# Table rows read two at a time and elsewhere, a fixed buffer for a chunk's first unit, and one instruction for two one-hots, in a two-layer graph network kernel

## The reference

```python
def _sage_conv(x, src, dst, W_l, b_l, W_r):
    msgs = x[src]
    agg = jax.ops.segment_sum(msgs, dst, num_segments=N_NODES)   # 12500 nodes
    deg = jax.ops.segment_sum(jnp.ones((src.shape[0],), x.dtype), dst, num_segments=N_NODES)
    mean = agg / jnp.maximum(deg, 1.0)[:, None]
    return mean @ W_l + b_l + x @ W_r
h = relu(_sage_conv(x, src, dst, W1_l, b1, W1_r))
h = relu(_sage_conv(h, src, dst, W2_l, b2, W2_r))
out = layernorm(x + h @ W3 + b3)
```

## Time and profile before

| | |
|---|---|
| Runs | 3, 3705.2 to 3718.2 us, median 3707.2 |
| The profiled execution | 3708.1 us; its span, first to last instruction, 3706.3 |
| TensorE | matmuls 2906.8 us (78%), weight loads 2393.2 (65%) |
| VectorE | 1475.7 us (40%), 3568 instructions |
| GpSimd | 2397.0 us (65%), 2448 of them gathers |
| ScalarE | 483.7 us (13%) |
| DMA | 653 MB, mean 176 GB/s |
| Granted TensorE clock | 0.897 of full speed over the span |

### The profile page before, as it was taken

How to read it: one execution, slowest core, us unless ns; L and a number is a source line. 1 busy time by engine, 2 the same in 40 slices (tenths; PEclk the granted TensorE clock), 3 DMA queues, 4 the chain that set the end, 5 groups by cost and what they waited for, 6 DMA issues and landing times.

```text
span 3706.3 us, 65299 instructions
## 1 busy us (share of the span) xinstructions
PE 2906.8 (78%) x13209; PEld 2393.2 (65%) x13210; DVE 1475.7 (40%) x3568; ACT 483.7 (13%) x1411; POOL 2397.0 (65%) x2455
## 2 busy tenths in 40 slices
PE   4777778788877878879865676888887888888866
PEld 2455667566656656768754565777776777777755
DVE  6555455445544444443222222333333333333332
ACT  2000000000000000010100111111112121121112
POOL 2556566556655666567655577777777777777765
PEclk7788899889989999989987888999999999999988
DMA  3234565557456556657655444776775766767665
GB/s 84 87 109 132 172 209 175 169 165 225 131 178 187 173 176 208 192 171 217 203 170 157 124 121 127 208 216 180 208 225 171 213 201 195 222 180 217 201 186 159
DMA packets 496459, 653.03 MB, mean 176 GB/s; under 512 B 184190, under 2 KB 414580, under 8 KB 493142
## 3 DMA queue, kind: packets, MB, share of 16 engines
q0 software_dynamic: 117504, 321.02, 29.4%
q1 hardware_dynamic: 298038, 254.08, 22.4%
q10 hardware_dynamic: 80800, 76.82, 6.8%
HBM read 581.29 MB, written 70.40 MB: 176 GB/s over the span
## 4 chain that ended last, share of the span: by engine, by line
PE 30%; POOL 21%; issue 16%; DVEq 12%; DMA 10%; DVE 6%; ACT 2%; PEld 1%; SPq 1%; PEldq 1%; ACTq 0%; POOLq 0%
POOL ring L406 21%; PE ps L486 15%; PE ps L545 7%; PE psY L588 3%; DMA counts<-scratch 3%; DMA ring<-z_rows,scol 3%; DVEq L886 2%; PE psY L577 2%; DVE oh L905 2%; DVEq L917 1%; DVE oh L907 1%; DMA scratch<-in_x 1%; DVE oh L874 1%; DMA work<-in_x 1%; DMA scratch<-z_rows 1%
## 5 line engine op out<-in xcount | busy, mean ns | idle before, releaser
L486 PE MATMUL ps<-ring,oh 128*125 128x257 f32 (+1 forms) x6416 | 1677.6, 417 | 501.0 <-DMA ring<-z_rows,scol 170.0
L486 PEld LDWEIGHTS ps<-ring,oh 128*125 128x125 f32 x6416 | 1291.0, 206 | 810.3 <-issue 597.8
L406 POOL DMA_INDIRECT ring<-in_x,scol x1224 | 1194.3, 976 | 850.9 <-PE ps L486 510.7
L406 POOL DMA_INDIRECT ring<-z_rows,scol x1224 | 1202.0, 982 | 435.3 <-issue 358.8
L874 DVE SCALAR_TENSOR_TENSOR oh<-dcol,cf,iota 128x500 f32<-128x500 int16 x802 | 594.1, 741 | 1319.3 <-PE ps L486 893.8
L545 PE MATMUL ps<-scratch 128*125 128x257 f32 (+1 forms) x2000 | 485.4, 391 | 14.0 <-DMA scratch<-in_x 14.0
L545 PEld LDWEIGHTS ps<-scratch 128*125 128x125 f32 x2000 | 460.4, 295 | 32.8 <-DMA scratch<-in_x 17.3
L861 DVE TENSOR_TENSOR acc<-ps,acc x806 | 337.3, 418 | 19.3 <-issue 15.3
L516 PE MATMUL psB<-oh 128*128 x540 | 180.2, 429 | 176.7 <-DVE oh L907 173.1
L1152 ACT COPY work<-psY 125x256 f32<-125x256 f32 x100 | 37.2, 372 | 1570.3 <-PE psY L577 1570.3
L516 PEld LDWEIGHTS psB<-oh 128*128 x540 | 53.7, 99 | 291.1 <-issue 267.2
(11 more groups left out here) (118 smaller groups left out, 1178.2 us busy)
## 6 DMA issues: line engine op xcount, KB each, us to landing
scratch<-counts SPq DMA_DIRECT2D x200, 312.5 KB
scratch<-in_x SPq DMA_DIRECT2D x114, 512.0 KB, 4.1
scratch<-z_rows SPq DMA_DIRECT2D x114, 512.0 KB, 4.3
counts<-scratch SPq DMA_DIRECT2D x25, 1250.0 KB
work<-in_x ACTq DMA_DIRECT2D x200, 125.0 KB
ring<-in_x,scol POOLq DMA_INDIRECT x1224
ring<-z_rows,scol POOLq DMA_INDIRECT x1224
scratch<-in_x SPq DMA_DIRECT2D x114, 128.0 KB, 6.4
```

Source lines behind the costliest of these rows:

```text
L406: pool.indirect_dma_start(ring[:, slot, b, 0:D], None, rows_dram, bass.IndirectOffsetOnAxis(scol[:, n - C0:n - C0 + 1], 0)).then_inc(rows[ ...
L486: mm = pe.matmul(psA[0:WN, bass.ds(bank, W)], oh[:, 2 * (slot % 2) + later, b, :], ring[:, slot, b, 0:W], start=(b == 0), stop=(b == nb - 1))
```

## The change

- `tab` has the words (first, lo = first + 1, end, until). The constant `blk` and its DMA are gone: the column is worked out from `ga` or `gb`. VectorE's setup has one more instruction of 306 words.
- A load brings eight words, the rows of two groups next to each other. `front` (groups i = 0 and 2) is loaded for the next four in group i = 3, `back` (i = 3 and 1) in group i = 0. The loads stand between the one-hot and the add on VectorE, and behind a group's first four products on TensorE. The `reg_add` to `lo` is gone.
- A chunk's row of `tabh` is loaded (`chunk_row`) in the group ahead of it, at the same place, instead of in `chunk`. The first chunks of a window have theirs ahead of `chunk` as before.
- SLOTS is 3. A chunk's first unit always uses place 0, without a wait. Later units use places 2 and 1 in turn (the counter is the loop's), and wait until all but the last unit have been multiplied (`s_cnt` starts at 2 and not at 4).
- One `tensor_tensor` over 2 x 128 columns makes both one-hots of 128, instead of two `tensor_scalar`. The two of 500 stay.
- The word of `win` for the next window is loaded at the end of `dense1`, and in `dense2` behind line 1022, instead of at their heads.

The diff, cut to its core (TensorE's `four_rows`, `row_of` and `chunk_row` are as VectorE's):

```diff
-SLOTS = 4
+SLOTS = 3
-            sp.dma_start(tab, c_tab).then_inc(s_w, 16)
...
+            def group(l, i, nb, builds=False):        # TensorE
+                lo, hi = row_of(i)[1:3]
+                pe.wait_ge(rows[l][i], pe.snap(turn, min_val=16, max_val=16 * GB * NGG))
+                pair(l, i, nb, 0)
+                if i == 0:
+                    four_rows(back, gb)
+                    pe.reg_add(gb, gb, -8)
+                if i == 3:
+                    pe.reg_add(ga, ga, 8)
+                    four_rows(front, ga)
+                if builds:
+                    chunk_row()
                 with pe.If(pe.snap(lo) < pe.snap(hi)):
                     with pe.Fori(pe.snap(lo, min_val=1, max_val=NW), pe.snap(hi, min_val=1, max_val=NW)):
-                        pair(l, slot, nb, 1)
-                pe.reg_add(gi, gi, -4 if i % 2 else 4)
+                        pair(l, i, nb, 1)
...
             def chunk(n):
-                pe.load([more], tabh[0:1, bass.ds(pe.snap(at_row, min_val=1, max_val=2 * (NH + NW) - 1), 1)])
-                pe.reg_add(at_row, at_row, 2)
-                count_blocks(n, True)
+                count_blocks(n, True, 0)
                 with pe.If(1 < pe.snap(more)):
-                    with pe.Fori(1, pe.snap(more, min_val=1, max_val=HB)):
-                        count_blocks(n, False)
+                    with pe.Fori(1, pe.snap(more, min_val=1, max_val=HB)) as j:
+                        pe.reg_alu(slot_at, j, 1, ALU.bitwise_and)
+                        pe.reg_alu(slot_at, slot_at, SW, ALU.mult)
+                        count_blocks(n, False, pe.snap(slot_at, min_val=0, max_val=SW) + SW)
...
+            def four_rows(row, at):                   # VectorE
+                v.load(row, tab[0:1, bass.ds(v.snap(at, min_val=0, max_val=(NGG - 2) * 4), 8)])
+            def row_of(i):
+                return (front[0:4], back[4:8], front[4:8], back[0:4])[i]
+            def mark_groups(l, i, nb, w, later, free):
                 at = (2 * (i % 2) + later) * OH
-                v.wait_ge(s_mm[l], v.snap(free, min_val=1, max_val=NG * NW + 2))
+                g = (ga, gb)[i % 2]
+                blk = v.snap(g, min_val=0, max_val=(NGG - 2) * 4) + (G0 * GB - C0 + (4 if i in (1, 2) else 0))
+                v.wait_ge(s_mm[l], free)
                 v.scalar_tensor_tensor(
...
-                add_product(l)
-                step(w)
-            def group(l, i, nb):
-                gi = (ga, gb)[i % 2]
-                v.load([first, hi, until, blk], tab[0:1, bass.ds(v.snap(gi, min_val=0, max_val=(NGG - 1) * 4), 4)])
-                v.reg_add(lo, first, 1)
-                pair(l, i, nb, v.snap(first, min_val=0, max_val=NW - 1), 0, c)
+            def group(l, i, nb, builds=False):
+                first, lo, hi, _ = row_of(i)
+                cv = v.snap(c, min_val=1, max_val=NG * NW + 1)
+                mark_groups(l, i, nb, v.snap(first, min_val=0, max_val=NW - 1), 0, cv)
+                if i == 0:
+                    four_rows(back, gb)
+                if i == 3:
+                    v.reg_add(ga, ga, 8)
+                    four_rows(front, ga)
+                if builds:
+                    chunk_row()
+                add_product(l, cv)
+                step(first)
...
-            def mark_blocks(n, base, table):
-                v.reg_alu(slot_at, slot_n, SW, ALU.mult)
-                to = v.snap(slot_at, min_val=0, max_val=(SLOTS - 1) * SW)
-                v.wait_ge(s_cnt, v.snap(hot, min_val=1, max_val=1 << 24))
+            def mark_blocks(n, base, table, to):
+                at = v.snap(hb, min_val=0, max_val=HK - 2)
+                s = oh1[:, bass.ds(to, SW)].rearrange("p (b n) -> p b n", b=2)
+                v.tensor_tensor(s[:, :, 0:P], iota[:, 0:P].unsqueeze(1).to_broadcast([P, 2, P]),
+                                key[:, 0, bass.ds(at, 2)].unsqueeze(2).to_broadcast([P, 2, P]), ALU.is_equal)
                 for b in range(2):
-                    at = v.snap(hb, min_val=0, max_val=HK - 2) + b
-                    v.tensor_scalar(oh1[:, bass.ds(to + b * (P + CJ), P)], iota[:, 0:P], key[:, 0, bass.ds(at, 1)],
-                                    None, ALU.is_equal)
-                    ins = v.tensor_scalar(oh1[:, bass.ds(to + b * (P + CJ) + P, n)], iota[:, table:table + n], base,
-                                          key[:, 1, bass.ds(at, 1)], ALU.add, ALU.is_equal)
+                    ins = v.tensor_scalar(s[:, b, P:P + n], iota[:, table:table + n], base,
+                                          key[:, 1, bass.ds(at + b, 1)], ALU.add, ALU.is_equal)
                 ins.then_inc(s_hot, 1)
                 v.reg_add(hot, hot, 1)
-                v.reg_add(slot_n, slot_n, 1)
-                v.reg_alu(slot_n, slot_n, SLOTS - 1, ALU.bitwise_and)
                 v.reg_add(hb, hb, 2)
...
             def chunk(n, base, table):
-                v.load([hb, more], tabh[0:1, bass.ds(v.snap(at_row, min_val=0, max_val=2 * (NH + NW) - 2), 2)])
-                v.reg_add(at_row, at_row, 2)
-                mark_blocks(n, base, table)
+                mark_blocks(n, base, table, 0)
                 with v.If(1 < v.snap(more)):
-                    with v.Fori(1, v.snap(more, min_val=1, max_val=HB)):
-                        mark_blocks(n, base, table)
+                    with v.Fori(1, v.snap(more, min_val=1, max_val=HB)) as j:
+                        v.reg_alu(slot_at, j, 1, ALU.bitwise_and)
+                        v.reg_alu(slot_at, slot_at, SW, ALU.mult)
+                        to = v.snap(slot_at, min_val=0, max_val=SW) + SW
+                        v.wait_ge(s_cnt, v.snap(hot, min_val=1, max_val=1 << 24))
+                        mark_blocks(n, base, table, to)
...
+            def next_range(i):
+                v.load([at_tile], win[0:1, bass.ds(i + 1, 1)])
```

129 lines of the change are left out of this document (70 added, 59 removed).

## The result

The median went from 3706.23 us (four runs, 3705.18 to 3718.18) to 3588.56 (four runs, 3583.82 to 3592.81): a ratio of 0.9675, with a 95% interval from 0.965 to 0.970, 118 us or 3.2% less. The profiled execution took 3591.78 us, its span is 3589.9.

A forecast was written before the change was run, and what follows sets the result against it. No engine was full in layer 1, they wait in turn; GpSimd's gathers lead layer 2. Terms 37 + 14 + 0 + 35 + 5 - 4 - 0.4 = 87 us, four fifths (69) arriving: 3638 us, range 3580 to 3695.

The forecast's parts named there:

- The loads of a group's row: Loads ahead of the one-hot removed, eight words at 0.40 us put back ahead of the add: net 37 us in layer 1.
- Layer 2's 14 us: Group-row loads in layer 2: 27 us removed from the chain, 13 us put back, net 14 us won.
- A chunk's row: Load of 533 ns moved from behind the copy to ahead of the add: 42 us less, 41 us back, net nothing.
- The one operation: VectorE's marking in layer 1: a unit takes 1.40 us against 1.56, over 218 units, 35 us won.
- The three places: Layer 1's chunks: the first unit's lost wait never held it, waits from the third unit on cost 4 us.
- TensorE's loads: 612 loads of 333 ns and 125 of 313 on TensorE's sequencer, covered by matmuls in both places: none counted.
- The window's word: 200 loads of 543 ns moved behind the mean, little of it on the chain: 5 us won, 0 to 12.
- I let four fifths arrive.: Of the 87 us summed, 69 us arrive, because other paths are close behind the chain.
- the loads only change places: Rival, 12%: VectorE's add is on the chain as often as its one-hot, so moved loads count in full; 3670 us.
- More than that arrives: Rival, 8%: the chunk's load is hidden and the loop of later units sheds its "issue" too; 130 us, 3577.
- A load is charged by the word: Rival, 4%, slower: eight words cost about 1.6 us, and TensorE's sequencer stands still at loads; 3827 us.
- The longer loop bodies: Rival, 3%, slower: more jumps leave what is fetched ahead, 0.5 us more at each of 306 groups, 150 us; 3780.

The follow-up runs named there:

- u3: c0 with a chunk's row loaded in the chunk again, behind the copy of the last counts: 3578.36 us, 0.9616 of the kernel before.
- d1: c0 with VectorE's eight-word loads written twice; the trace shows no second loads. On the slower chip: 4238.45 us, 0.9622 of the kernel before.
- c0: The changed kernel with one register move replaced (fin = max(until, 0)), base of the follow-up runs: 3582.5 us, 0.9628 of the kernel before.
- b1: The kernel before with only the one operation for the two one-hots of 128: 3637.63 us, 0.9803 of the kernel before.
- b2: The kernel before with only the fixed place for a first unit, no wait there, loop's counter for later ones: 3656.07 us, 0.9865.
- u4: c0 with the ring of four places and a wait ahead of every unit again, on both engines: 3618.15 us, 0.9745 of the kernel before.
- u2: c0 with a group's four words loaded at its head again, on both engines: 3595.06 us, 0.9667 of the kernel before.
- n2: c0 with the windows' words on partition 32, beside the chunks' rows, instead of 64. On the slower chip: 4219.56 us, 0.9601 of the kernel before.
- b4: The kernel before with the one operation and the fixed place, loads as before. On the slower chip: 4273.52 us, 0.9726 of the kernel before.
- b3: The kernel before with only the loads moved as in the change. On the slower chip: 4359.78 us against 4395.03, 0.9918.
- u1: c0 with a unit's two one-hots of 128 made by two operations again: 3595.78 us, 0.9656 of the kernel before.
- n1: c0 with VectorE's row loads behind a chunk's last marking instead of between one-hot and add: 3618.89 us, 0.9758 of the kernel before.

## Why the prediction was right, and where it was not

The forecast was 3638 us with a range of 3580 to 3695; 3588.6 came. Direction, stage and range hold; the size does not (118 us for 69), and several terms were wrong in ways that offset one another. That the time lies in the range, 9 us from its lower end, is in part luck: the loads were given too much, the marking a third of what it brought, and the range was drawn for other reasons.

- **The loads of a group's row.** "I take 0.40": eight words take 0.60, and 0.82 behind a window's word. The step that failed is the line through one and four words, 7 ns a word: four words cost as much as one, eight cost 0.27 more than four. So the 612 loads of 0.35 became 308 that cost nearly as much in all (278 and 257 us over the run). That the new place delays the add was right: at the median it starts 1.29 us behind the one-hot where one load stands between, 1.79 with two and 0.66 with none; I had said 1.1. That the place is charged in full fits what the runs show: 150 us more from one-hot to add in the stage, and in u3 79 us less there against 94 more in the chunks with the same time in the end. d1, which was to price it directly, can't.
- **Layer 2's 14 us.** None came: its length is 1643.4 us, in c0 1642.1, against 1637.2 before. The step that failed is the reading of 1.1% of the chain as removable; GpSimd's gathers stood ready to take the share and did.
- **A chunk's row.** "Net nothing" is right, and by the mechanism given: the first marking follows at 0.60 us as forecast, the add takes it back, and u3 shows 0.1% of no certain sign. Only the delay of the add was put too low, 1.29 for 1.1.
- **The one operation.** I took 0.45 for the `tensor_tensor`; 0.418 is the mean. The Trainium skill's formula for an fp32 `tensor_tensor` (VectorE: DVE Perf Modes, the errata section) makes an estimate of 0.424; the trace agrees. Two `tensor_scalar` of 128 took 2 x 0.267, so the engine's own work shrank too, by 0.12 us a unit. The term of 35 us was the mis-sized one: alone the operation gave 71. In b1 a chunk is 0.60 us shorter, 0.28 for each of its 2.16 units, where I had 0.16, and all 270 units pay, where I had 218. With all parts a chunk's second unit starts 0.97 us behind its first at the median and a third 1.12 behind the second (1.57 and 1.39 before), and not 1.40. The step that failed is "from the last marking's start to the next unit 0.67 with one register operation less": at the median it is 0.78 before, 0.63 in b1 and 0.32 with all parts, where the next unit starts as the last marking ends. I added the sequencer's time behind the engine's. The rows fit two that run beside each other, of which the larger counts.
- **The three places.** "The first unit loses a wait that never held it" is right, and "I take 4 us" of cost is wrong: undoing it costs 1.2%, doing it alone gives 53 us. What was missed is not time spent waiting but the sequencer's work for the ring, 0.55 us a chunk on VectorE in b2, while its sequencer is the slower one, 0.21 in u4, and 0.2 us on TensorE's.
- **TensorE's loads.** "I count none" is wrong behind a chunk: there the sequencer isn't ahead, and the load at the group's head stood open, 0.52 us (u2).
- **The window's word.** It now costs a change of partition twice; n2, which takes that away, can't be told from d1 (0.9601 and 0.9622).
- **"I let four fifths arrive."** Of VectorE's 257 us in chunks 107 arrived. The reason is not other paths but above all the loads' new place, which the table above prices at 150 us.

The rival **"the loads only change places"** had the mechanism of the loads: they bring about 1%, 30 to 40 us, of the 56 that I had for them with the window's word, and undone one by one in the changed kernel hardly anything (u2 0.4%, u3 nothing). The rest of the gain is marking, 2.7% or 100 us by b4, of which I had 31. **"More than that arrives"** (3577) came nearest to the number, though its first ground failed: the chunk's load isn't hidden in its new place. **"A load is charged by the word"** fell: eight words cost 0.60 us and not 1.6. The Trainium skill's figure for a load of registers, about 200 ns for each even in bulk (Runtime: NRT & Kernel Launch, Instruction fetch mechanics), would make it 1.6 as well, an estimate; the trace disagrees for these tables in SBUF. **"The longer loop bodies"** (150 us more, which makes 3788 and not 3780) fell too: the kernel got faster, and the queue that brings instructions moved 80 packets for 99.

Of the theories in the expectations, that one part alone brings the gain is out: b1, b2 and b3 each bring a piece. The picture of the overlap holds where it is put to the test most sharply: the one operation, 2.0% alone, is worth 0.3% on top of the others. It holds less well elsewhere. The fixed place is worth 1.35% alone and 1.2% on top, where the picture wants less, and place and loads together (u1) give 3.4%, more than their 1.35% and 0.8% alone. Possible reasons are the bases (the kernel before took 3719.51 us beside c0 and u1 to u3, and 3708.95 beside u4, b1, b2 and n1, 0.3% apart), b3's other chip, and TensorE's two shortened steps; none was tried apart.

## What to carry to other kernels

An engine with idle gaps marked "issue" and hardly a busy sequencer row is likely bound by its sequencer: count register operations and instructions there, and take the larger of sequencer time and engine time for each stretch, not their sum. A load on VectorE's sequencer cost time wherever it stood in layer 1: ahead of the first marking and ahead of the add it cost the same in the end (u3), and two in a row behind the markings cost more (n1). What pays is an instruction or a counter less (b1, b2). Before a run that adds work is read as free, its trace has to show the added work (d1). Time taken out of one place of the same sequencer is to be looked for at the place where it was put before it is called a gain.

## What the hardware showed beyond that

- Register loads from SBUF: one word 0.31 us, four 0.33 to 0.35, eight 0.59 to 0.61; two words on VectorE take 0.53 to 0.54, more than four. Why two words cost that was not tried.
- On VectorE a load costs 0.22 us more when the one before it read on the other side of the border between partition 64 and partitions 0 and 32 (eight words 829 ns at the median for 609, in the changed kernel); between 0 and 32 it is within 10 ns. n2 takes it away by placement.
- A load does not wait for the operation that runs: in the kernel before 67 of the 125 loads of a chunk's row ran wholly beneath a VectorE operation, at 530 ns for a median of 533 over all.
- One chip ran the kernel before in 4395.03 us, 18 to 19% above the others, with a mean clock of 0.848 to 0.868 in the kernels profiled there. Single operations and loads took as long as elsewhere at the median. Part of the extra time shows as single long stalls: of the 145 steps from a last marking to the next unit 17 are over 2 us in d1, the longest 9.3, and one in c0, with 0.33 and 0.32 at the median. What causes them stays open.
